# Score groups ordered by query half, and the order of the side work placed anew, in a one-core attention and expert kernel

## The reference, cut to what matters

```python
scores = einsum('bthd,bshd->bhts', q, k) / sqrt(128)
A = scores * exp(G[t] - G[s]) * lamw[t, s]        # for s <= t only; lamw: softplus of a level of t - s
y = einsum('bhts,bshd->bthd', A, v)
out = y @ Wo.T + xn                               # xn: the normalised x
x = x + layernorm(out) * ln_g + ln_b
gate = softmax(layernorm(x) @ Wg + bg)            # two largest, renormalised
x = x + sum_e gate[e] * (layernorm(x) @ We[e].T + be[e])
```

## Time and profile before

| | before |
|---|---|
| time, median of 3 runs | 1462.64 us (1460.75 to 1463.16) |
| the profiled execution: time / span | 1460.58 us / 1458.8 us |
| TensorE, VectorE, ScalarE, GpSimd busy | 95%, 71%, 79%, 64% |
| granted TensorE clock, mean | 0.993 |

### The profile page before, as it was taken

The page is one execution under the profiler, slowest core; times in us unless marked ns, Lnnn a source line. Parts: engine busy times, 40 slices in busy tenths (PEclk is TensorE's granted clock), DMA queues, the critical chain, the costliest instruction groups (busy, mean ns, idle before and its releaser), DMA issues.

```text
span 1458.8 us, 30735 instructions
## 1 busy us (share of the span) xinstructions
PE 1390.9 (95%) x10478; PEld 1166.3 (80%) x10478; DVE 1041.8 (71%) x2445; ACT 1157.7 (79%) x3412; POOL 933.1 (64%) x1018
## 2 busy tenths in 40 slices
PE   5899999999999999999999999999999999999997
PEld 5687888878878788887888788887887878878875
DVE  4767666797767877687766976668776796667667
ACT  3789888887889778897788877889778987877742
POOL 2355569655696567955588556974569655696573
PEclk9999999999999999999999999999999999999998
DMA  5311111111211122011121011110211011111100
GB/s 190 72 18 18 31 19 32 18 23 40 40 9 17 24 40 40 18 11 38 25 40 14 17 34 23 39 18 18 45 24 23 17 24 26 39 18 19 24 8 15
DMA packets 256342, 44.05 MB, mean 30 GB/s; under 512 B 197960, under 2 KB 254522, under 8 KB 256058
## 3 DMA queue, kind: packets, MB, share of 16 engines
q1 hardware_dynamic: 253980, 41.69, 15.1%
q10 hardware_dynamic: 2206, 0.40, 0.2%
HBM read 32.31 MB, written 9.18 MB: 28 GB/s over the span
## 4 chain that ended last, share of the span: by engine, by line
PE 56%; POOL 18%; DVE 11%; ACT 9%; issue 3%; SPq 1%; DMA 0%; ACTq 0%; POOLq 0%; DVEq 0%
PE o_ps L1429 15%; POOL a_lo L615 9%; PE l_ps L1366 7%; PE s_ps L1345 5%; PE s_ps L1347 5%; PE s_ps L1346 5%; ACT w_all L769 5%; PE aux L1345 4%; PE aux L1347 4%; PE aux L1346 4%; DVE a_all L988 3%; ACT a_hi L791 2%; DVE z L1064 2%; POOL late L640 2%; POOL e_rs L621 2%
## 5 line engine op out<-in xcount | busy, mean ns | idle before, releaser
L615 POOL TENSOR_TENSOR a_lo<-a_all,a_hi 128x512 fp32r<-128x512 f32 (+2 forms) x640 | 719.4, 1139 | 476.8 <-ACT a_hi L791 474.6
L769 ACT ACTIVATE w_all<-l_ps,bias 128x128 f32<-128x128 f32 x2287 | 624.4, 388 | 22.5 <-PE l_ps L1366 21.0
L988 DVE TENSOR_TENSOR a_all<-s_ps,w_all 128x512 f32<-128x512 f32 (+3 forms) x768 | 419.7, 553 | 259.7 <-PE s_ps L1347 219.5
L791 ACT ACTIVATE a_hi<-a_all 128x512 fp32r<-128x512 f32 (+2 forms) x640 | 359.7, 595 | 196.1 <-DVE a_all L988 194.9
L1429 PE MATMUL o_ps<-a_hi,v_all 128*128 128x512 f32 (+2 forms) x1280 | 463.4, 367 | 11.1 <-POOL a_lo L615 11.1
L1429 PEld LDWEIGHTS o_ps<-a_hi,v_all 128*128 128x128 f32 x1280 | 240.8, 188 | 49.0 <-POOL a_lo L615 11.8
L1345 PE MATMUL s_ps<-q_hi,xt_hi 128*128 128x512 f32 (+2 forms) x640 | 258.6, 404 | 7.8 <-DVE a_all L988 7.0
L1347 PE MATMUL s_ps<-q_hi,xt_lo 128*128 128x512 f32 (+2 forms) x640 | 230.9, 361 | 0.0
L1346 PE MATMUL s_ps<-q_lo,xt_hi 128*128 128x512 f32 (+2 forms) x640 | 230.5, 360 | 0.0
L1429 PE MATMUL o_ps<-a_lo,v_all 128*128 128x512 f32 (+2 forms) x640 | 229.5, 359 | 0.0
L1366 PE MATMUL l_ps<-rb,mask 96*128 96x64 f16 (+1 forms) x1774 | 143.9, 221 | 11.4 <-ACT w_all L769 11.2
(11 more groups left out here) (234 smaller groups left out, 2118.7 us busy)
## 6 DMA issues: line engine op xcount, KB each, us to landing
rb<-eb_scratch SPq DMA_DIRECT2D x1016, 0.8 KB
ra<-ea_scratch SPq DMA_DIRECT2D x508, 4.0 KB, 2.0
mt<-m_scratch SPq DMA_DIRECT2D x62, 128.0 KB, 2.1
nt<-n_scratch SPq DMA_DIRECT2D x62, 128.0 KB, 2.6
tx<-in_L_attn_x SPq DMA_DIRECT2D x9, 512.0 KB, 4.2
out<-late SPq DMA_DIRECT2D x15, 256.0 KB, 2.8
late<-in_L_attn_x SPq DMA_DIRECT2D x7, 512.0 KB, 4.2
ea_scratch<-tx SPq DMA_DIRECT2D x15, 128.0 KB
```

The source lines that it names most:

```text
L615: pool.tensor_tensor(a_lo[r][:, 0:t1 - t0], a[r][:, 0:t1 - t0], a_hi[r][:, 0:t1 - t0].bitcast(F32), ALU.subtract).then_inc(a_lo_done, 1)
L769: last = act.activation(w[k][:, W_AT[j] + dd, :].rearrange("p (f c) -> p f c", f=2), l_tiles[:, :, :, i - i0], ACT.Exp, bias=bias[b % 2][: ...
L791: act.activation(a_hi[r][:, 0:t1 - t0], a[r][:, 0:t1 - t0], ACT.Copy).then_inc(a_hi_done, 1)
L988: dve.tensor_tensor(a[(n * NG + g) % NA][:, 0:t1 - t0], s_ps[:, g % 2, 0:t1 - t0], w[n % 2][:, at:at + (t1 - t0) // P, :].rearrange("p i n ...
```

## The change

The groups are ordered by query half: widths 512, 384, 256, 128 for half 0 and then 512 five times, 384, 256, 128 for half 1. So half 0 of `o_ps` is complete after slot 3 of a sequence's last head (its values come at slot 8), not after slot 6. `scores` and `values` find the first group of each half by `FIRST_OF` (slots 0 and 4). All tables of side work are written anew; `UNITS`, `U_AT`, `LAG` and the instructions of every piece stay. In the tail VectorE makes statistics, means and products of half 0 before it takes half 1 of `o_ps`, and goes through half 0 to its shifts before it begins half 1; GpSimd makes second deviations of half 0 before first ones of half 1; TensorE transposes half 0 of y before its last five `values`; the fillers go from 46, 6, 3 to 22, 22, 3.

```diff
 GROUPS = []
-for _j in range(NC):
-    for _lo in (0, T // 2):
+for _lo in (0, T // 2):
+    for _j in range(NC):
         _a = max(_j * P, _lo)
         if _a < _lo + T // 2:
             GROUPS.append((_j, _a, _lo + T // 2))
 NG = len(GROUPS)
+FIRST_OF = [[_a // (T // 2) for _j, _a, _b in GROUPS].index(f) for f in range(2)]
...
-Q_AT = {7: 0, 20: 1}
-V_AT = {8: 0, 22: 1, 37: 2, 44: 3}
+Q_AT = {5: 0, 21: 1}
+V_AT = {11: 0, 22: 1, 40: 2, 46: 3}
...
-PE_MORE = {10: [('Y', 0)], 24: [('Y', 1)], 74: [('T', 0)], 88: [('Z', 0)], 104: [('T', 1)], 122: [('X', 0)],
-           133: [('X', 1)], 137: [('Z', 1)], 141: [('L', 0)], 173: [('H', 0)], 200: [('G', 0)], 205: [('H', 1)],
+PE_MORE = {9: [('Y', 0)], 24: [('Y', 1)], 66: [('T', 0)], 80: [('Z', 0), ('T', 1)], 124: [('X', 0)], 128: [('Z', 1)],
+           132: [('X', 1)], 145: [('L', 0)], 173: [('H', 0)], 194: [('G', 0)], 205: [('H', 1)], 217: [('EL', 0)],
...
-DVE_MORE = {13: [('t_stat', 2), ('t_stat', 1), ('t_stat', 0)], 20: [('t_stat', 3)], 21: [('o', 1)],
+DVE_MORE = {16: [('t_stat', 2), ('t_stat', 1), ('t_stat', 0)], 20: [('t_stat', 3)], 21: [('o', 1)],
...
-            192: [('softplus', 1), ('guard', 0)], 201: [('sums', 0)], 208: [('log', 0)], 209: [('log', 1)],
-            212: [('up', 1)], 221: [('decay', 0)], 225: [('l_low', 0), ('up', 2)], 236: [('up', 3)],
+            192: [('softplus', 1), ('guard', 0)], 200: [('sums', 0)], 204: [('log', 0)], 208: [('up', 1)],
+            220: [('log', 1)], 225: [('l_low', 0), ('up', 2)], 236: [('up', 3)], 240: [('decay', 0)],
...
-            352: [('up', 14)], 376: [('up', 15)], 383: [('o', 0)]}
+            352: [('up', 14)], 372: [('up', 15)], 376: [('o', 0)]}
...
-            145: [('exp', 0)], 170: [('ln', 0)], 189: [('lnl', 0)], 220: [('l_high', 0)], 240: [('l_high', 1)]}
-POOL_MORE = {25: [('t_dev', 0)], 32: [('xb', 0)], 36: [('dev1', 0)], 44: [('apply1', 1)], 45: [('apply1', 0)],
-             52: [('apply1', 2)], 65: [('xb', 1), ('apply1', 3), ('scale', 0)], 69: [('scale', 1)], 77: [('add', 0)],
-             81: [('add', 1)], 89: [('dev2', 0)], 101: [('apply2', 1)], 113: [('apply2', 3)], 273: [('total', 0)], 321: [('base', 0)],
-             369: [('total', 1)], 376: [('base', 1)]}
+            149: [('exp', 0)], 158: [('ln', 0)], 190: [('lnl', 0)], 214: [('l_high', 0)], 240: [('l_high', 1)]}
+POOL_MORE = {9: [('t_dev', 0)], 29: [('xb', 0)], 41: [('dev1', 0)], 45: [('apply1', 1)], 49: [('apply1', 0)],
+             52: [('apply1', 2)], 61: [('apply1', 3)], 65: [('scale', 0), ('scale', 1)], 72: [('xb', 1)],
+             77: [('add', 0)], 80: [('add', 1)], 97: [('dev2', 0)], 109: [('apply2', 1)], 113: [('apply2', 2)],
+             277: [('total', 0)], 321: [('base', 0)], 372: [('total', 1)], 376: [('base', 1)]}
...
                 for f in range(2):
                     first_deviation(B - 1, f)
-                for f in range(2):
                     second_deviation(B - 1, f)
...
-                for i0 in range(0, HC, 2):
-                    first_statistics(B - 1, i0)
-                take_o(B - 1, 1)
-                first_mean(B - 1, 0)
-                last_sums(0)
-                for i0 in range(HC, NC, 2):
-                    first_statistics(B - 1, i0)
-                first_mean(B - 1, 1)
-                last_sums(1)
                 for f in range(2):
+                    for i0 in (f * HC, f * HC + 2):
+                        first_statistics(B - 1, i0)
+                    first_mean(B - 1, f)
+                    last_products(f)
+                    if f == 0:
+                        take_o(B - 1, 1)
+                    last_sums(f)
                     for i0 in (f * HC, f * HC + 2):
                         second_statistics(B - 1, i0)
                     second_mean(B - 1, f)
-                for f in range(2):
                     for i in range(f * HC + 2, (f + 1) * HC):
                         last_shift(i)
...
+                turn_y(B - 1, 0)
                 for g in range(NG - LAG, NG):
                     values(NH - 1, g)
-                    if g == NG - LAG:
-                        turn_y(B - 1, 0)
                 pe.wait_ge(a_done, NH * NG)
-                idle = {("Y", 1): 46, ("X", 0): 6, ("X", 1): 3}
+                idle = {("Y", 1): 22, ("X", 0): 22, ("X", 1): 3}
```

More of the change, by code:

```diff
@@ new lines @@
+V_AT = {11: 0, 22: 1, 40: 2, 46: 3}
+Q_OUT = {9: 0, 23: 1}
+V_HIGH = {10: 0, 25: 1, 40: 2, 44: 3}
+V_LOW = {14: 0, 31: 1, 41: 2, 52: 3}
+PE_MORE = {9: [('Y', 0)], 24: [('Y', 1)], 66: [('T', 0)], 80: [('Z', 0), ('T', 1)], 124: [('X', 0)], 128: [('Z', 1)],
[4 rows of a table added]
+DVE_MORE = {16: [('t_stat', 2), ('t_stat', 1), ('t_stat', 0)], 20: [('t_stat', 3)], 21: [('o', 1)],
+            25: [('stat1', 1)], 33: [('stat1', 0)], 45: [('stat1', 2), ('stat1', 3)], 69: [('t_low', 0)],
+            80: [('z', 0)], 92: [('stat2', 0), ('stat2', 1), ('stat2', 2)], 97: [('t_low', 1)], 104: [('stat2', 3)],
+            132: [('x_low', 0)], 137: [('z', 1)], 141: [('x_low', 1)], 145: [('gate', 0)], 152: [('gate', 1)],
+            160: [('gate', 2)], 180: [('gate', 3)], 181: [('up', 0)], 189: [('softplus', 0)],
+            192: [('softplus', 1), ('guard', 0)], 200: [('sums', 0)], 204: [('log', 0)], 208: [('up', 1)],
+            220: [('log', 1)], 225: [('l_low', 0), ('up', 2)], 236: [('up', 3)], 240: [('decay', 0)],
[3 rows of a table added]
@@ new lines @@
+ACT_MORE = {2: [('y', 0)], 33: [('y', 1)], 41: [('t_apply', 0)], 44: [('t_apply', 1), ('t_apply', 3)],
+            54: [('t_apply', 2)], 66: [('t_high', 0)], 88: [('t_high', 1)], 116: [('apply2', 0)],
+            124: [('x_high', 0), ('apply2', 3)], 134: [('x_high', 1)], 144: [('abs', 0)], 145: [('num', 0)],
+            149: [('exp', 0)], 158: [('ln', 0)], 190: [('lnl', 0)], 214: [('l_high', 0)], 240: [('l_high', 1)]}
[3 more added lines that the diff above has]
+             277: [('total', 0)], 321: [('base', 0)], 372: [('total', 1)], 376: [('base', 1)]}
@@ L1083, in first_mean, with last_products @@
                     mean_var(dve, b, part, e_st1, e_mv1, e_ve1, e["st1"], e["mv1"], e["ve1"])
+                def last_products(f):
+                    for i in range(f * HC, (f + 1) * HC):
+                        dve.scalar_tensor_tensor(yn[:, i, :], yn[:, i, :], e_mv1[:, 0, i:i + 1], lng, ALU.add,
+                                                 ALU.mult).then_inc(e["r0"], 1)
                 def last_sums(f):
                     b = B - 1
-                    tiles = range(f * HC, (f + 1) * HC)
-                    for i in tiles:
-                        dve.scalar_tensor_tensor(yn[:, i, :], yn[:, i, :], e_mv1[:, 0, i:i + 1], lng, ALU.add,
-                                                 ALU.mult).then_inc(e["r0"], 1)
                     dve.wait_ge(e["rs1"], upto(b, f))
                     dve.wait_ge(e["xb"], 2 * b + f + 1)
-                    for i in tiles:
+                    for i in range(f * HC, (f + 1) * HC):
                         dve.wait_ge(e["r0"], NC * b + i + 1)
@@ L1412, in values @@
                     r, vr = (n * NG + g) % NA, n % 3
-                    fresh = h == 0 and g < 2
+                    fresh = h == 0 and g in FIRST_OF
                     if fresh and b:
-                        pe.wait_ge(y_done, 2 * (b - 1) + g + 1)
+                        pe.wait_ge(y_done, 2 * (b - 1) + FIRST_OF.index(g) + 1)
                     elif fresh:
```

14 lines of the change are left out of this document (2 added, 12 removed), and 10 rows, old and new, of tables (DVE_MORE, PE_MORE).

## The result

| | before | after |
|---|---|---|
| time, median of 7 runs each | 1461.5 us (1460.75 to 1463.16) | 1456.89 us (1455.2 to 1458.81) |
| ratio, 95% interval | | 0.9965 [0.9955, 0.9975] |
| the profiled execution: time / span | 1460.58 / 1458.8 us | 1456.01 / 1454.1 us |
| granted TensorE clock, mean | 0.993 | 0.991 |
| first execution of a unit 0 in head 8 | 212.03 us | 213.80 us |

What follows compares the result with a forecast made beforehand. TensorE's own work plus 4.85 us of waits a sequence bounds the body, GpSimd's list and the chain behind it the tail. Body -0.35 x 7 = -2.45, tail -0.85, sum -3.3 from 1462.64: 1459.3 us, range 1450 to 1471.

Steps and rivals of the forecast that it cites:

- the sign of being wrong: Sequence period off by over 0.5 us, with a_lo waits in head 1 (slower) or none in heads 3 and 4 (faster).
- Head 4, unit 1: Body: the unit comes 0.9 us sooner, so its wait for unit 0's exponentials grows from 0.66 to 1.0 us.
- Head 3, logarithm: Body, ScalarE: moved between exponentials of units 1 and 2, it makes the waits 1.4 us where they were 1.08.
- Level logs: Body, VectorE: parting the two steps leaves a wait of 0.6 us before slot 9's scores, instead of 1.04 + 0.29.
- GpSimd in heads 0 and 1: Body: `t_dev` moves early and slot 9's subtraction precedes `dev1`; waits 1.3 us a sequence against 1.59, bounds 0 and 4.4.
- Everything else moved costs nothing: Body: the other moved pieces stand in slots without waits, hidden under TensorE, cost 0; uncovered, each costs 0.6 to 1.4 us.
- Tail, the list of last subtractions: Tail, GpSimd: same 15.9 us of work, only the 0.25 us wait for the last add_up goes: -0.25.
- Behind `take_o`: Tail: the chain to half 1's turn shortens from 15.05 to 14.45 us, -0.60, with a new wait of 1.85 before `last_shift`.
- that does not move `take_o`: Tail: half 0's earlier statistics, means and products leave `take_o` in place, since it hangs on GpSimd's last subtractions.
- The rival with slow fillers: Tail: the second 22 fillers at 0.43 us hold half 1's turn to 17.9, +3.4, giving 1462.7 us; chance 0.05.
- GpSimd becomes the bound in heads 0 and 1: Rival, body: GpSimd idles for statistics, then has five subtractions in a row; +8.6, giving 1471.2 us; chance 0.20.
- The waits mostly go: Rival, body: bunched pieces are apart, GpSimd keeps its deadlines, the logarithm is absorbed; -10, giving 1452.7 us; chance 0.24.

Runs made afterwards that it cites:

- seventh experiment: The changed kernel with the logarithm of head 3 back on ScalarE at place 170 instead of 158: 1465.1 us, ratio 1.0021 to before.
- tenth: The changed kernel with VectorE's two level logs side by side again at places 208 and 209, add_up at 212: 1458.51 us, ratio 0.997 to before.
- third experiment: The changed kernel's body with the former tail: former order on VectorE, GpSimd and TensorE, former fillers: 1453.57 us, ratio 0.9951 to before.
- ninth: The changed kernel with ScalarE's `t_apply` of tile 0 at place 43 instead of 41, behind unit 4's exponentials: 1456.94 us, ratio 0.9966 to before.
- twelfth: Changed kernel, tail gap filled, last two x shifts a head sooner, `t_apply` at 43, statistics of tiles 4, 5 at 96: 1454.35 us, 0.9938 to before.
- first experiment: The new order of groups with the side-work tables and tail of before: 1493.55 us, ratio 1.0221 to before.
- second experiment: The former order of groups with the new side-work tables and the tail of before: 1479.02 us, ratio 1.0121 to before.
- sixth: The kernel before with GpSimd's `dev1` at place 41 instead of 36, behind slot 9's subtraction: 1462.11 us, ratio 0.9999.
- fourth experiment: The changed kernel with VectorE's statistics, means and products of half 1 before half 0's shifts, fillers 22, 14, 3: 1454.4 us, ratio 0.9945 to before.
- fifth experiment: The kernel before with its two level logs apart at places 204 and 220, sums at 200, decays at 240: 1472.6 us, ratio 1.0067.

## Why the prediction was right, and where its sum was off

The sign and the time held (1459.3 forecast, 1456.89 measured), with two errors that partly cancel: body 2.7 us too little, tail 1.3 us too much. That is in good part luck. The forecast had the body's gain in heads 0 and 1 (-0.3) and next to none in heads 3 to 7 (-0.07); it was the other way about, +0.24 in heads 0 to 2 and -1.2 in heads 3 to 7. The forecast's period was 173.8 and the measured one 173.17, so off by more than the 0.5 that it had named as the sign of being wrong, though neither pattern of waits that it named with it came.

- *Head 4, unit 1, from 0.66 to 1.0*: measured 0.85. Right in sign, 0.15 over.
- *Head 3, logarithm, from 1.08 to 1.4*: measured 1.10. The comparison with before was the wrong one to draw the edit's worth from: the new order brings the unit sooner, so at the former place the wait is larger (seventh experiment). The edit saves 0.7. In the profile after, the logarithm follows its table load at once (load at 1151.53 for 1.28, logarithm at 1152.82), as in the earlier trace rows. The Trainium skill, ScalarE: Activation LUTs, What ACT_TABLE_LOAD costs, has a drain of about 1380 ns on top; this trace doesn't show one. (The 20 us that the prediction works out from it are the edit's cost alone; less the 3.3 the change would have lost some 16.)
- *Level logs, from 1.33 to 0.6* (its own terms, 5.1 less 4.35, give 0.75): none of their waits is left in the list, where I put 0.6. Undone, it costs 0.4 a sequence (tenth), and not in the waits that I priced but in the head behind them; 0.7 was forecast.
- *GpSimd in heads 0 and 1, from 1.59 to 1.3*: `t_dev` began 8.9 us after head 0's first scores (forecast 9.2) and the list behind it ended at 25.8 (forecast 26.5), and slot 9's wait went, as said. (The forecast's start of head 0 before, 1081.7, was 0.7 late; the scores begin at 1081.01. Counted its way it is 8.3 and 25.2.) But I compared waits, and the run of GpSimd as a whole sets these heads. The sum that holds is idle time of GpSimd ahead of its run, 2.64 before and 2.88 after: +0.24, not -0.3.
- *Everything else moved costs nothing*: this step failed. 1.07, 0.81 and 0.38 came from pieces that I had put at 0, since the rows of before showed no wait in their slots. For the time it did no harm: the first two lie inside GpSimd's run and took the place of others (ninth and twelfth).
- *The body's rest*: heads 3 to 7 gave 1.2 us a sequence where 3.07 against 3.0 was forecast. Single undoings account for 0.7 (logarithm) and 0.4 (level logs), which is nearly all.
- *Tail, the list of last subtractions, -0.25*: measured +0.25. GpSimd's stretch without a gap is shorter as said (15.85 against 16.14), but it begins 0.54 later against unit 0 of head 62, behind a wait of 1.61 for a_hi where 0.55 stood before. *Behind `take_o`, -0.60*: measured -0.47, with the new wait of 1.8 as said. The number is right by luck: the former order gives 17.64 with the new body (third experiment), so the new order gave nothing here, +0.07. The 0.54 under before is the fillers' clock in before's execution; the 46 fillers held its transposes, which the forecast's chain left out. *What failed* is "that does not move `take_o`": statistics, means and products of half 0 come before it on VectorE, and they ended at 1415.8, and `take_o` stands 0.66 further behind GpSimd's last subtraction than before. Two of the means' instructions, of four columns, took 1.25 and 0.76 where such instructions take 0.16.
- *The fillers*: 22 of them took 7.17 (forecast 6.2) and the next 22 took 4.91 (4.7). The rival with slow fillers is false: the second lot ended 0.5 before the turn.

Of the rivals, "GpSimd becomes the bound in heads 0 and 1" had the mechanism, but GpSimd was the bound before too; a new order with unsuited places (first experiment) is what it looks like when it costs. "The waits mostly go" was half right: it is what happened in heads 4 and 5, and can't happen in heads 0 to 2 while GpSimd's run is as long.

What stays open: whether GpSimd's 2.9 us of idle time in head 0 (2.15 for a_hi, 0.73 for statistics) can be filled too. By the rule it is what could shorten heads 0 to 2 without less work for GpSimd. It wasn't tried. Open too is what the 0.4 us are that heads 3 to 7 gained outside the listed waits, and whether the wait of 1.53 is all that the second experiment has over the rule.

## What to carry to other kernels

Before you price single waits of the critical engine, look for a run without gaps on another engine of the same stretch: there the waits only change places (three kernels here, the sixth, ninth and twelfth, removed 0.7 to 1.6 us of them for nothing), and what counts is that engine's idle time ahead of the run. An order of work and a table of places fitted to it are one thing: each half alone cost 1.2 to 2.2%, both together gave 0.35%. When a wait is forecast in a chain, look for independent work queued behind it: moving that ahead gave 2.1 us here, more than twice what the reordered tail itself was meant to give. And run the new part with the old one beside it: only the third experiment showed that the -0.47 behind `take_o`, which matched the forecast, was not the new order's.

## What the runs showed that was not expected

**Small VectorE instructions stood still beside GpSimd.** L443 and L444 take two inputs of 128 x 4 from the same memory and last 0.16 us elsewhere in the tail. Beside GpSimd's L677 (1412.14 to 1413.42) L443 lasted from 1412.19 to 1413.44, and beside the subtraction (1413.38 to 1414.11) L444 from 1413.37 to 1414.13: each ended with GpSimd's instruction. In the fourth experiment one lasted 1.93 over two of them. The statistics ahead of them, with one input, took 0.87 beside GpSimd's subtraction, as they do elsewhere in the tail. The Trainium skill, SBUF — State Buffer, section SBUF: two separate sides, says that a VectorE instruction with two inputs from SBUF and a GpSimd instruction that reads SBUF exclude each other for the whole of the one that starts first. The trace agrees in the lengths (the second pair starts within 0.01 us, so which was first can't be read); I had not applied it to instructions so small, and it cost 1.7 us ahead of `take_o`, of which 0.66 showed.

**TensorE's granted clock fell in single heads, and the sum of the waits doesn't tell it.** Head 27 of the first experiment:

```profile
638.66:663.13 24.47, 22.68 (x163) 18.86 (x162) 20.50 (x47) 22.39 (x57) 11.45 (x10) 0.93 0.08 9
```

At 2.4 GHz throughout, the same head of another sequence took 22.88. The mean of 0.93 means a part at 1.2 GHz, though TensorE was busy for 22.68 of the 24.47 us. Seven heads of that kernel had it, eight of the fifth experiment, none of before or of the third and fourth, one (head 0) of after. Held beside the same head without it, a drop made its head, or two neighbours together, 1.3 to 1.6 us longer. In the first experiment the next head was 1.1 to 1.4 shorter for it; in the fifth nothing came back, and its three sequences took 7.4 us more in all. So a single execution can be off by more than the edit under study. It didn't go with the length of the waits: the longest wait in the six sequences was 1.46 us in the fifth experiment and 1.40 in before, and the seventh has one of 2.30 in each of the six and a drop in one. What triggers it wasn't found.
